# Last headed attention's opening re-ordered, its weights fetched by two queues, its output bias added by groups

## The chip, the cores and the metric

One core of a Trainium2 chip runs the whole program in one launch. The metric is the device time of one execution in microseconds (us), the median over several executions. Everything is in 32-bit floats where the text says nothing else.

## The reference, cut to what matters

The program is a stack of four layers on a stream of 2 x 1024 tokens of width 256. Each layer has a cross attention to 77 context tokens (or a self attention) and a feed-forward part. What is changed is the cross attention of the last layer, with 16 heads of 16, which reads a normalised copy of the stream and adds its result back:

```
def _L3_xattn_ref(q, k, v, mask, wq, bq, wk, bk, wv, bv, wo, bo):
    Q = (q @ wq + bq).reshape(b, s, 16, 16).transpose(0, 2, 1, 3)
    K = (k @ wk + bk)...            # k and v are the context, 77 tokens
    V = (v @ wv + bv)...
    score = jnp.einsum('bhqd,bhkd->bhqk', Q, K) / np.sqrt(16)
    score = jnp.where(mask, NEG, score)
    attn = jax.nn.softmax(score, axis=-1)
    x = jnp.einsum('bhqk,bhkd->bhqd', attn, V) ...
    return x @ wo + bo
...
x = x + _L3_xattn_ref(_layernorm(x, axis=-1), ctx_1024, ctx_1024, mask, ...)
x = x + _L3_ffn_ref(_layernorm(x, axis=-1), ...)     # 8 experts, each token goes to one
```

## The kernel before

The stream lies in SBUF as `x_resid`, 16 tiles of 128 tokens, in four groups of four tiles (`NCH` is 4, a group is 512 tokens). A stage is a block with one instruction stream for each engine. The streams are written out by hand, and semaphores tie them together. The page's engine names are PE (TensorE), DVE (VectorE), ACT (ScalarE), POOL (GpSimd) and SP (SyncE).

The stage before the change is the third layer's routed feed-forward. It ends with four DMAs on SP's queue that read the stream back into `x_resid`, one for each group (line 1970, 512 KB each).

The stage of the change is `headed_cross_attention` with the name `a3` (the page shortens its tensors to `a_...`). The same function serves the second layer, named `a1`, where there is a bias tensor instead of a mask, no arrivals and no projection bias. It has an opening and a loop over the 16 tiles. These are the steps of the opening before the change:

- SP's queue: `headed.fetch` issues the loads of `wk`, `wv`, two small selection tables, `bk`, `bv`, `bq`, `wq`, the mask (2048 rows of 77 bytes), `wo` and `bo` in that order, all counted on one semaphore. `w.wait` waits until all of them are in. Then come the next stage's small parameters, a wait for the four groups of the stream, and six loads of 1 MB each, the first three experts' weights (lines 395 and 396).
- PE: 16 matmuls that compute nothing that is used (`keep_busy`, line 76), `turn_tokens(0)` (transposes of group 0, line 1204), `w.wait`, the keys' projection (line 1251), `values(0)`, `turn_tokens(1)`, `values(1)`, `queries(0)` (line 1214), `turn_tokens(2)`, `queries(1)`, `scores(0)` (line 1224), `turn_tokens(3)`, `queries(2)`, `scores(1)`, `queries(3)`. A 32-bit matmul shows as two records, a transpose as one.
- DVE: statistics of the four groups (line 1019), `normed_tokens` (line 1009: subtract the mean, multiply by the root) of groups 0, 1 and 2, with `block_keys` (line 996), the evictions `tokens_turned` (line 1013) and `limits` (the mask turned into a limit, lines 1002 and 1003) between, `normed_tokens(3)`, then `scores` (line 1038) and `maxima` (line 1043) of tiles 0 and 1.
- POOL: four small copies and a memset, the roots of the variances by groups (lines 921 and 923), `w.wait`, for each of two batches the value bias (lines 934 to 940), then one addition of `bo` to all 16 tiles of `x_resid` (line 944), which waits until all 16 tiles are normed because the norm reads the same tensor, then `below_maximum(0)` (line 949).
- ACT: an exponential that warms its table (line 1136), evictions of transposes (1117), `w.wait`, evictions of values (1133, 1134) and of queries with their bias (1124).

The loop begins on PE with `scores(2)`, once the last query eviction on ACT is through and the six value steps on POOL are. For each tile it computes the scores two tiles ahead, transposes the exponentials, multiplies with the values and projects with `wo`. Its operations are untouched.

Of the kernel before, what the change touches and what calls it, by code (L numbers as in the profile page):

```python
# [5 lines left out]
ALU = mybir.AluOpType  # L6
# [5 lines left out]
U8 = mybir.dt.uint8  # L12
AX = mybir.AxisListType.X

P = 128
# [84 lines left out]
def bcast(ap, n):  # L100

    return ap.unsqueeze(0).broadcast_to([n] + list(ap.shape))
# [11 lines left out]
class Loads:  # L114
# [12 lines left out]
        self.at[n] = ap  # L127
        self.total += 16

    def fetch(self, eng, n, source):  # L130
        if self.target is None:
            self.counter[1] += self.total
            self.target = self.counter[1]
        eng.dma_start(self.at[n][:], source).then_inc(self.arrived, 16)

    def wait(self, eng):
# [659 lines left out]

class HeadedWeights:

    def __init__(self, core, ctx, name, counter, wqT, wkT, wvT, woT, mask=None, bq=None, bk=None, bv=None, bo=None):
        self.dram, self.loads = core.dram, Loads(core, ctx, name, counter)  # L800
        self.wqT, self.wkT, self.wvT, self.woT, self.mask = wqT, wkT, wvT, woT, mask
        self.bq, self.bk, self.bv, self.bo = bq, bk, bv, bo
        self.biased = bq is not None
        place = self.loads.place
        for n in ("wk", "wv", "wq", "wo"):
            place(n, [P, KD, D])
        place("head_of", [P, 8])
        place("rest_of", [8 * REST, 8])
        if self.biased:
            place("bq", [P, KD])  # L810
            place("bk", [P, KD])
            place("bv", [P, D])
            place("bo", [P, D])
        if mask is not None:
            place("mask", [P, NT, KEYS], U8)

    def fetch(self, sp):
        fetch = self.loads.fetch
        fetch(sp, "wk", self.wkT.rearrange("(k p) d -> p k d", p=P))
        fetch(sp, "wv", self.wvT.rearrange("(k p) d -> p k d", p=P))  # L820
        fetch(sp, "head_of", self.dram["head_of"])
        fetch(sp, "rest_of", self.dram["rest_of"])
        if self.biased:
            fetch(sp, "bk", self.bk)
            fetch(sp, "bv", bcast(self.bv, P))
            fetch(sp, "bq", self.bq)
        fetch(sp, "wq", self.wqT.rearrange("(k p) d -> p k d", p=P))
        if self.mask is not None:
            fetch(sp, "mask", self.mask.rearrange("(t p) k -> p t k", p=P))
        fetch(sp, "wo", self.woT.rearrange("(k p) d -> p k d", p=P))  # L830
        if self.biased:
            fetch(sp, "bo", bcast(self.bo, P))

    def wait(self, eng):
        self.loads.wait(eng)

    def __getitem__(self, n):
        return self.loads[n]


def headed_cross_attention(core, name, w, out, bias=None, arrivals=None, fetch=None, stream=None, experts=None, early=0):
# [8 lines left out]
    with ExitStack() as ctx:  # L850
# [59 lines left out]
        def _(pool):  # L910
# [6 lines left out]
            if arrivals is not None:  # L917
                for g in range(NCH):
                    own = slice(4 * g, 4 * g + 4)
                    pool.wait_ge(moments_done, 4 * g + 4)  # L920
                    pool.tensor_scalar(rstd[:, own], moments[:, own, 1], EPS, None, ALU.add).then_inc(eps_done, 1)
                    pool.wait_ge(eps_done, g + 1)
                    pool.tensor_tensor(rstd[:, own], rstd[:, own], half[:].broadcast_to([P, 4]), ALU.pow).then_inc(rstd_done, 1)
                pool.wait_ge(rstd_done, NCH)
# [16 lines left out]
            if projection_bias:  # L941
                pool.wait_ge(normed, NT)
                pool.wait_ge(v_sb, 3 * BATCH)
                pool.tensor_tensor(out[:], out[:], w["bo"][:].unsqueeze(1).broadcast_to([P, NT, D]), ALU.add).then_inc(biased, 1)

            def below_maximum(t):
                pool.wait_ge(max_done, t + 1)
# [14 lines left out]
            below_maximum(0)  # L962
            for t in range(NT):
                if t + 1 < NT:
                    below_maximum(t + 1)
# [12 lines left out]
        def _(dve):  # L978
# [6 lines left out]
                dve.wait_ge(chain, count[0])  # L985

            def block_keys():
                w.wait(dve)
                link(dve.tensor_reduce(quarter_of[:], head_of[:].rearrange("p (j h) -> p h j", h=2), AX, ALU.max))
                link(dve.tensor_scalar(quarter_of[:], quarter_of[:], DK ** -0.5, None, ALU.mult))  # L990
                dve.wait_ge(kv_mm, 1)
                for k in range(KD):
                    keys = ps[:, k, 0:W].rearrange("p (b n) -> p b n", b=BATCH)
                    for h in range(2):
                        if projection_bias:
                            dve.tensor_scalar(kbd[:, :, k, h, :], keys, bkT[:, k:k + 1], quarter_of[:, h:h + 1], ALU.add, ALU.mult).then_inc(kbd_done, 1)
                        else:
                            dve.tensor_scalar(kbd[:, :, k, h, :], keys, quarter_of[:, h:h + 1], None, ALU.mult).then_inc(kbd_done, 1)

            def limits():  # L1000
# [69 lines left out]
                dve.bn_aggr(moments[:, t, :], stats[:, t, :]).then_inc(out_moments, 1)  # L1070

            if arrivals is not None:
                for g in range(NCH):
                    statistics(g)
            normed_tokens(0)
            normed_tokens(1)
            tokens_turned(0)
            normed_tokens(2)
            block_keys()
            tokens_turned(1)  # L1080
            limits()
            normed_tokens(3)
            tokens_turned(2)
            scores(0)
            maxima(0)
            tokens_turned(3)
            scores(1)
            maxima(1)
# [25 lines left out]
        def _(act):  # L1114
# [13 lines left out]
            def values(b):  # L1128
# [57 lines left out]
        def _(pe):  # L1186
# [60 lines left out]
            turn_tokens(0)  # L1247
            w.wait(pe)
            for k2 in range(KD):
                for k in range(KD):  # L1250
                    mm = pe.matmul(ps[:, k2, 0:W], w["wk"][:, k, k2 * P:(k2 + 1) * P], core.ctxT[:, k, :], start=(k == 0), stop=(k == KD - 1))
            mm.then_inc(kv_mm, 1)
            values(0)
            turn_tokens(1)
            values(1)
            queries(0)
            turn_tokens(2)
            queries(1)
            pe.wait_ge(kbd_done, 2 * KD)
            pe.wait_ge(v_raw, 3 * BATCH)  # L1260
            scores(0)
            turn_tokens(3)
            queries(2)
            scores(1)
# [1703 lines left out]
def program(nc, dram):  # L2968
    with ExitStack() as ctx:
# [46 lines left out]
        with ExitStack() as routed:  # L3016
# [2 lines left out]
            experts.keep(routed, 3)  # L3019
            with ExitStack() as layer:  # L3020
                headed = HeadedWeights(core, layer, "a3", "a0o", *(dram[f"L3_w{n}"] for n in "qkvo"), mask=dram["mask_bf"],
                                       bq=dram["L3_bq"], bk=dram["L3_bk"], bv=dram["L3_bv"], bo=dram["L3_bo"])
                headed.fetch(nc.sync)
# [93 lines left out]
```

## Time and profile before

| | us |
|---|---|
| median of 3 runs (2120.34 to 2125.79) | 2125.45 |
| profiled execution, its own time | 2126.2 |
| its span | 2124.4 |
| PE busy | 1987.4 |
| this stage's opening, from PE's first instruction to its loop | 1821.77 to 1858.81 |

Times in the trace count from the start of the span. A row of the timeline gives the start, the length, the engine, the line, what is written and what is read, and in brackets how long the engine had been idle and what released it. DMA rows on a queue (SPq) give the time that the issue took, not the transfer.

### The profile page before, as it was taken

To read this page: it belongs to the slowest core of one execution; us is meant where nothing else is said; L and a number is where in the kernel's file an instruction comes from. 1 tells how busy PE (TensorE), PEld (TensorE's weight loads), DVE (VectorE), ACT (ScalarE), POOL (GpSimd) and SP (SyncE) were. 2 spreads that over 40 slices of the span, in tenths; PEclk is the share of its full clock that TensorE was granted. 3 is DMA by queue.
4 is the path that set the end of the run, shared out by engine and by line. 5 is a ranking of instruction groups with operands and counts; after the bars stand their busy time and mean duration, and the time that the engine had idled before them with its cause. 6 is when DMAs were issued, how large, how long until landed. Compare 5 with 4: busy or idle time off the path is not lost. (4 is left out here: it accounts for less than half of the span.)

```text
span 2124.4 us, 39759 instructions
## 1 busy us (share of the span) xinstructions
PE 1987.4 (94%) x12589; PEld 1455.5 (69%) x12590; DVE 1047.7 (49%) x2419; ACT 931.7 (44%) x1932; POOL 722.1 (34%) x814
## 2 busy tenths in 40 slices
PE   6899999988999999879999978999999999798998
PEld 5576656742333232469999867999999999565898
DVE  6885853677777777353222255222222222487221
ACT  2422652157777777523333332333333333265222
POOL 0122973520000000234333342434333343585433
PEclk9999999999999999999999988999999999999999
DMA  5003300042111112155222164522222222602721
GB/s 171 21 1 129 124 13 0 1 155 72 39 43 48 45 39 60 63 178 168 32 33 35 27 206 145 147 35 34 33 36 38 35 33 32 191 22 62 232 35 23
DMA packets 124860, 150.44 MB, mean 71 GB/s; under 512 B 27638, under 2 KB 105303, under 8 KB 124749
## 3 DMA queue, kind: packets, MB, share of 16 engines
q1 hardware_dynamic: 93981, 116.61, 17.0%
q0 software_dynamic: 24288, 31.81, 9.4%
q8 instruction: 64, 1.05, 0.2%
q10 hardware_dynamic: 6480, 0.59, 0.2%
q14 instruction: 47, 0.39, 0.1%
HBM read 113.33 MB, written 37.38 MB: 71 GB/s over the span
## 5 line engine op out<-in xcount | busy, mean ns | idle before, releaser
L2102 PE MATMUL banks<-m_rowsT,x_normT 128*128 128x128 f32 x4032 | 471.2, 275 | 4.5 <-ACT m_hT L2341 2.0
L2102 PEld LDWEIGHTS banks<-m_rowsT,x_normT 128*128 128x128 f32 x4032 | 461.8, 192 | 18.9 <-ACT m_hT L2341 2.4
L2111 PE MATMUL banks<-m_experts,m_hT 128*128 x2016 | 455.8, 380 | 0.0
L2111 PEld LDWEIGHTS banks<-m_experts,m_hT 128*128 128x128 f32 x2016 | 374.0, 190 | 45.2
L2341 ACT ACTIVATE m_hT<-banks,m_bias 128x128 f32<-128x128 f32 x848 | 241.7, 368 | 245.0 <-PE banks L2102 241.3
L2017 POOL DMA_INDIRECT scratch_acc<-m_y,m_row_ids x106 | 170.2, 1606 | 398.2 <-ACT m_y L2351 357.4
L2812 ACT ACTIVATE sh_pT<-banks 128x1024 f32<-128x1024 f32 x256 | 250.8, 1024 | 27.0 <-PE banks L2773 27.0
L2290 DVE COPY m_rowsT<-banks 128x256 f32<-128x256 f32 x88 | 37.4, 425 | 409.7 <-PE banks L2093 409.7
L2351 ACT ACTIVATE m_y<-banks,m_weight 128x256 f32<-128x256 f32 x126 | 59.6, 473 | 351.8 <-PE banks L2114 289.0
L2836 DVE TENSOR_REDUCE sh_mhalf<-banks 128x1 f32<-128x512 f32 x308 | 194.3, 684 | 36.4 <-PE banks L2722 36.4
L2274 DVE TENSOR_SCALAR x_normT<-m_experts 128x2048 f32 x129 | 168.1, 1303 | 74.0 <-issue 69.5
L2773 PE MATMUL banks<-sa_qs,sa_ks 99*128 99x512 bf16 x512 | 153.8, 385 | 9.7 <-ACT sh_pT L2812 7.5
L2004 POOL DMA_INDIRECT m_rows<-scratch_rows,m_row_ids x114 | 127.1, 1115 | 99.2 <-POOL m_row_ids L2001 97.0
L2713 POOL TENSOR_TENSOR x_norm<-x_norm,sp_bo 128x256 f32<-128x256 f32 x16 | 11.6, 724 | 389.6 <-DVE sh_m L2846 389.6
L2722 PE MATMUL banks<-sa_ks,sa_qs 96*128 96x512 bf16 x410 | 136.0, 387 | 0.0
L2763 PE MATMUL banks<-sh_pT,sa_vh 128*17 128x512 f32 x1024 | 132.1, 598 | 1.2 <-ACT sh_pT L2812 1.2
L76 PE MATMUL banks<-ident 128*128 128x256 f32 x336 | 92.9, 429 | 32.4 <-PEq L1847 18.0
L2773 PEld LDWEIGHTS banks<-sa_qs,sa_ks 99*128 99x128 bf16 x512 | 41.5, 98 | 116.7 <-ACT sh_pT L2812 51.0
L2286 DVE TENSOR_SCALAR m_rowsT<-banks,m1p_gain,m1p_shift 128x128 f32<-128x128 f32 x76 | 27.7, 406 | 177.1 <-PE banks L2093 177.1
L76 PEld LDWEIGHTS banks<-ident 128*128 128x128 f32 x336 | 70.7, 218 | 47.6 <-issue 35.5
L2722 PEld LDWEIGHTS banks<-sa_ks,sa_qs 96*128 96x128 bf16 x410 | 40.3, 98 | 77.0 <-DVE sh_mhalf L2836 35.6
L2841 DVE CUSTOM_DVE_ANT_0 sh_rise<-banks,sh_rise 128x512 f32<-128x512 f32 x102 | 68.4, 689 | 34.5 <-ACT sh_rise L2800 33.3
(413 smaller groups left out, 2766.5 us busy)
## 6 DMA issues: line engine op xcount, KB each, us to landing
m_experts<-L_W SPq DMA_DIRECT2D x32, 1024.0 KB
m_experts<-L1f_W SPq DMA_DIRECT2D x16, 1024.0 KB
a_bt<-bias SPq DMA_DIRECT2D x16, 616.0 KB, 3.8
scratch_parts<-sp_part SPq DMA_DIRECT2D x16, 384.0 KB, 2.5
sa_qs<-scratch_parts SPq DMA_DIRECT2D x96, 64.0 KB, 2.3
scratch_rows<-x_norm SPq DMA_DIRECT2D x12, 512.0 KB, 3.9
sa_ks<-scratch_parts SPq DMA_DIRECT2D x90, 64.0 KB, 2.3
scratch_acc<-x_resid SPq DMA_DIRECT2D x8, 512.0 KB, 2.9
```

The source lines that it names most:

```text
L76: pe.matmul(self.ps[:, bank, 0:2 * P], self.ident[:], self.ident[:].unsqueeze(1).broadcast_to([P, 2, P]), start=True, stop=True)
L2004: pool.indirect_dma_start(rows[:, w % RING, :], None, table, bass.IndirectOffsetOnAxis(ap=row_ids[:, w:w + 1], axis=0), bounds_check=TOK, ...
L2017: pool.indirect_dma_start(stream, bass.IndirectOffsetOnAxis(ap=row_ids[:, w:w + 1], axis=0), y[:, w % RING, :], None, bounds_check=TOK - 1 ...
L2102: mm = pe.matmul(ps[:, H_BANK[u] + f // 4, f % 4 * P:(f % 4 + 1) * P], w1_tile[:, u, k, f * P:(f + 1) * P], rowsT[:, u, k, :], start=(k == ...
L2111: mm = pe.matmul(ps[:, Y_BANK[u], 0:D], hT[:, u, f, :], experts.w2[:, bass.ds(slot_of(e), 1), f, :], start=(f == 0), stop=(f == FB - 1 and ...
L2274: ins = dve.tensor_scalar(w1_tile[:, u, :, :], experts.w1[:, bass.ds(slot_of(e), 1), :, :].rearrange("p e k f -> p (e k) f"), 0.0, None, A ...
L2341: ins = act.activation(hT[:, u, f, :], ps[:, H_BANK[u] + c, j * P:(j + 1) * P], func, bias=bias[:, u, f:f + 1])
L2722: pe.matmul(ps[:, bank["a", s, c], :], qs[u][0:SR, h, t * P:(t + 1) * P], keys, start=True, stop=True).then_inc(a_mm, 1)
L2763: mm = pe.matmul(ps[32 * g:32 * g + DK + 1, O_BANK, :], vh[:, b * KT + k, head, :], pT[:, (2 * k + h) % 4, half, :], start=(k == 0), stop= ...
L2773: mm = pe.matmul(ps[:, B_BANK + 2 * (n % 2) + half, :], ks[u][:, h, k * P:(k + 1) * P], qs[u][:, h, half * CH:(half + 1) * CH], start=True ...
L2812: act.activation(pT[:, n % 4, :, :], ps[:, B_BANK + 2 * (n % 2):B_BANK + 2 * (n % 2) + 2, :], ACT.Exp, scale=DK ** -0.5).then_inc(exp_done, 1)
L2836: dve.tensor_reduce(mhalf[:, s % 2, half, col:col + 1], ps[:, bank["a", s, c], :], AX, ALU.max).then_inc(a_max, 1)
```

## The change

`HeadedWeights` now holds two sets. The set of the keys (`wk`, `wv`, the two tables, `bk`, `bv`) stays on SP's queue; the others (`wq`, `bq`, the mask, `wo`, `bo`) are issued by ACT, ahead of its table load, and are counted on a second semaphore (`others="a0v"`). `expect` sets a set's target without issuing. For the second layer both sets stay on SP with one semaphore, and its order is kept.

```diff
+    def wait_of_keys(self, eng):
+        (self.others if self.together else self.of_keys).wait(eng)
...
             def limits():
+                w.wait(dve)
...
-            w.wait(pool)
-            for b in range(BATCH):
+            def values(b):
...
-                pool.tensor_tensor(out[:], out[:], w["bo"][:]....broadcast_to([P, NT, D]), ALU.add).then_inc(biased, 1)
+            def add_output_bias(g):
+                own = slice(4 * g, 4 * g + 4)
+                pool.wait_ge(normed, 4 * g + 4)
+                pool.tensor_tensor(out[:, own], out[:, own], w["bo"][:]....broadcast_to([P, 4, D]), ALU.add).then_inc(biased, 1)
...
+                roots(0)
+                roots(1)
+                roots(2)
+                w.wait_of_keys(pool)
+                w.wait(pool)
+                add_output_bias(0)
+                values(0)
+                roots(3)
+                add_output_bias(1)
+                add_output_bias(2)
+                add_output_bias(3)
+                below_maximum(0)
+                values(1)
```

DVE's opening in this stage (`block_keys` waits for the keys' set alone):

```diff
-                for g in range(NCH):
-                    statistics(g)
-            normed_tokens(0)
...
+                statistics(0)
+                statistics(1)
+                normed_tokens(0)
+                statistics(2)
+                tokens_turned(0)
+                normed_tokens(1)
+                block_keys()
+                statistics(3)
+                tokens_turned(1)
+                normed_tokens(2)
+                normed_tokens(3)
+                limits()
+                tokens_turned(2)
+                scores(0)
+                maxima(0)
+                scores(1)
+                maxima(1)
+                tokens_turned(3)
...
-                dve.wait_ge(biased, 1)
+                dve.wait_ge(biased, NCH)
```

ACT and PE:

```diff
+            if arrivals is not None:
+                w.fetch_others(act)
             act.activation(warm[:], half[:], ACT.Exp)
             tokens_turned(0)
-            w.wait(act)
             values(0)
             tokens_turned(1)
             values(1)
+            w.wait(act)
             queries(0)
...
-            core.keep_busy(pe, 7, 16 if arrivals is not None else 5)
...
+                core.keep_busy(pe, 7, 10)
+                keys()
+                turn_tokens(0)
+                values(0)
+                turn_tokens(1)
+                values(1)
+                w.wait(pe)
+                queries(0)
+                turn_tokens(2)
+                pe.wait_ge(q_sb, KD)
+                pe.wait_ge(kbd_done, 2 * KD)
+                pe.wait_ge(v_raw, 3 * BATCH)
+                scores(0)
+                queries(1)
+                turn_tokens(3)
+                scores(1)
+                queries(2)
...
             queries(3)
```

`keys()` is the former keys' projection with a wait for the keys' set alone. In `program`, `headed.fetch(nc.sync)` becomes `headed.fetch_of_keys(nc.sync)` and `headed.others.expect()`.

## Rows read from the trace of the kernel before

**Rows 1.** The page, busy time of each engine and its share of the span.
```profile
PE 1987.4 (94%) x12589; PEld 1455.5 (69%) x12590; DVE 1047.7 (49%) x2419; ACT 931.7 (44%) x1932; POOL 722.1 (34%) x814
```

**Rows 2.** Windows: stretch, length, busy time by engine, granted clock, DMA share, GB/s.
```profile
1834.12:1857.07 22.95, 22.95 (x112) 13.41 (x112) 14.78 (x23) 8.26 (x16) 17.61 (x11) 1.00 0.77 274
...
1858.81:1945.13 86.32, 79.61 (x800) 53.80 (x800) 66.34 (x138) 54.31 (x110) 76.18 (x69) 1.00 0.06 20
```

**Rows 3.** Timeline of PE and of ACT's last query evictions in the opening.
```profile
1821.77 9.84 PE L76 MATMUL banks<-ident 128*128 128x256 f32 x32 [9.93 <-PEq L1847]
...
1831.45 1.04 PE L1204 MATMUL banks<-ident,x_norm 128*128 128x128 f32 x8
...
1834.12 1.32 PE L1251 MATMUL banks<-ctxT_sb,a_wk 128*128 128x154 f32 x8 [1.64 <-DMA a_bo<-L_bo]
...
1853.37 3.70 PE L1214 MATMUL banks<-x_normT,a_wq 128*128 128x512 f32 x8
...
1857.51 1.24 ACT L1124 ACTIVATE a_qT<-banks,a_bq 128x512 f32<-128x512 f32 x2
1858.81 0.81 PE L1224 MATMUL banks<-a_kbd,a_qT 32*128 32x154 f32 x16 [1.74 <-ACT a_qT L1124]
```

**Rows 4.** Timeline of the queue of SP.
```profile
1826.39 4.01 SPq L134 DMA_DIRECT2D a_wo<-L_wo  x1
...
1832.06 0.37 SPq L395 DMA_DIRECT2D m_experts<-L_W  x1
```

**Rows 5.** Windows of the reload and the weights, columns as in rows 2.
```profile
1821.73:1831.61 9.88, 9.84 (x34) 8.23 (x35) 8.37 (x39) 1.49 (x2) 7.08 (x13) 0.72 1.15 304
...
1826.50:1827.00 0.50, 0.50 (x2) 0.35 (x2) 0.50 (x2) 0.00 (x0) 0.33 (x2) 0.50 1.11 348
...
1830.00:1830.50 0.50, 0.50 (x4) 0.45 (x3) 0.50 (x3) 0.00 (x0) 0.42 (x2) 1.00 1.54 129
```

**Rows 6.** Line 2437, issues by ACT: ns min/median/max, first and last start.
```profile
L2437 ACTq DMA_DIRECT2D sa_ks<-scratch_parts x6: 357/1143/1208, 472.5 to 477.6; - x6
```

**Rows 7.** Timeline of DVE in the opening.
```profile
1823.24 1.41 DVE L1019 BATCH_NORM_STATS2 stats<-x_resid 128x6 f32<-128x256 f32 x4 [23.21 <-DMA x_resid<-scratch_acc]
...
1833.13 1.37 DVE L1009 TENSOR_SCALAR x_norm<-x_resid,moments,rstd 128x256 f32<-128x256 f32 x4
...
1838.68 0.79 DVE L1002 TENSOR_SCALAR a_bt<-a_mask 128x1232 f32<-128x1232 uint8 x1
...
1841.13 2.53 DVE L1009 TENSOR_SCALAR x_norm<-x_resid,moments,rstd 128x256 f32<-128x256 f32 x4
...
1848.31 1.51 DVE L1038 TENSOR_TENSOR a_s<-banks,a_bt 128x616 f32<-128x616 f32 x2 [3.51 <-PE banks L1224]
1849.85 1.44 DVE L1043 TENSOR_REDUCE a_mx<-a_s 128x16 f32<-128x1232 f32 x1
1851.21 0.68 DVE L1013 COPY x_normT<-banks 128x512 f32<-128x512 f32 x1
```

**Rows 8.** Timeline of POOL in the opening.
```profile
1829.72 0.30 POOL L921 TENSOR_SCALAR rstd<-moments 128x4 f32<-128x4 f32 x1 [0.22 <-DVE moments L1022]
1830.11 1.16 POOL L923 TENSOR_TENSOR rstd<-rstd,minus_half 128x4 f32<-128x4 f32 x1
1838.36 1.44 POOL L934 TENSOR_TENSOR a_v_main<-a_v_main,a_bv 64x128 f32<-64x128 f32 x2 [7.09 <-ACT a_v_rest L1134]
1839.87 1.80 POOL L937 TENSOR_TENSOR a_v_rest<-a_v_rest,a_bv 104x256 f32<-104x256 f32 x1
...
1842.52 0.99 POOL L934 TENSOR_TENSOR a_v_main<-a_v_main,a_bv 64x128 f32<-64x128 f32 x2
1845.16 8.87 POOL L944 TENSOR_TENSOR x_resid<-x_resid,a_bo 128x4096 f32<-128x4096 f32 x1
1853.98 2.25 POOL L949 TENSOR_TENSOR a_s<-a_s,a_mx 128x1232 f32<-128x1232 f32 x1
```

**Rows 9.** A window ahead of the stage, columns as in rows 2.
```profile
1816.50:1817.00 0.50, 0.00 (x0) 0.00 (x0) 0.00 (x0) 0.00 (x0) 0.00 (x0) 0.99 1.14 76
```

More of the change, by code:

```diff
@@ L797, with __init__ @@
 class HeadedWeights:
-    def __init__(self, core, ctx, name, counter, wqT, wkT, wvT, woT, mask=None, bq=None, bk=None, bv=None, bo=None):
-        self.dram, self.loads = core.dram, Loads(core, ctx, name, counter)
+    def __init__(self, core, ctx, name, counter, wqT, wkT, wvT, woT, mask=None, bq=None, bk=None, bv=None, bo=None, others=None):
+        self.dram, self.of_keys, self.others = core.dram, Loads(core, ctx, name, counter), Loads(core, ctx, f"{name}o", others or counter)
         self.wqT, self.wkT, self.wvT, self.woT, self.mask = wqT, wkT, wvT, woT, mask
@@ L802, in __init__ @@
         self.bq, self.bk, self.bv, self.bo = bq, bk, bv, bo
[L803 to L808, printed above, removed]
+        self.biased, self.together = bq is not None, others is None
+        self.of_keys.place("wk", [P, KD, D])
+        self.of_keys.place("wv", [P, KD, D])
+        self.others.place("wq", [P, KD, D])
+        self.others.place("wo", [P, KD, D])
@@ L809, in __init__ @@
+        self.of_keys.place("head_of", [P, 8])
+        self.of_keys.place("rest_of", [8 * REST, 8])
         if self.biased:
[L810 to L813, printed above, removed]
+            self.others.place("bq", [P, KD])
+            self.of_keys.place("bk", [P, KD])
+            self.of_keys.place("bv", [P, D])
+            self.others.place("bo", [P, D])
         if mask is not None:
-            place("mask", [P, NT, KEYS], U8)
@@ L817, in fetch @@
[L817 to L822, printed above, removed]
-        if self.biased:
[L824 to L827, printed above, removed]
+            self.others.place("mask", [P, NT, KEYS], U8)
@@ new lines, in fetch_of_keys, with fetch_others @@
+    def fetch_of_keys(self, eng):
+        fetch = self.of_keys.fetch
+        fetch(eng, "wk", self.wkT.rearrange("(k p) d -> p k d", p=P))
+        fetch(eng, "wv", self.wvT.rearrange("(k p) d -> p k d", p=P))
+        fetch(eng, "head_of", self.dram["head_of"])
+        fetch(eng, "rest_of", self.dram["rest_of"])
+        if self.biased:
+            fetch(eng, "bk", self.bk)
+            fetch(eng, "bv", bcast(self.bv, P))
+    def fetch_others(self, eng):
+        fetch = self.others.fetch
+        fetch(eng, "wq", self.wqT.rearrange("(k p) d -> p k d", p=P))
+        if self.biased:
+            fetch(eng, "bq", self.bq)
@@ L834, in wait @@
     def wait(self, eng):
-        self.loads.wait(eng)
+        self.others.wait(eng)
+    def wait_of_keys(self, eng):
+        (self.others if self.together else self.of_keys).wait(eng)
     def __getitem__(self, n):
-        return self.loads[n]
+        return self.of_keys[n] if n in self.of_keys.at else self.others[n]
 def headed_cross_attention(core, name, w, out, bias=None, arrivals=None, fetch=None, stream=None, experts=None, early=0):
@@ L916, in _, with roots @@
             pool.wait_ge(zeros_done, 1)
-            if arrivals is not None:
-                for g in range(NCH):
[L919 to L924, printed above, removed]
-            w.wait(pool)
-            for b in range(BATCH):
+            def roots(g):
+                own = slice(4 * g, 4 * g + 4)
+                pool.wait_ge(moments_done, 4 * g + 4)
+                pool.tensor_scalar(rstd[:, own], moments[:, own, 1], EPS, None, ALU.add).then_inc(eps_done, 1)
+                pool.wait_ge(eps_done, g + 1)
+                pool.tensor_tensor(rstd[:, own], rstd[:, own], half[:].broadcast_to([P, 4]), ALU.pow).then_inc(rstd_done, 1)
+            def values(b):
                 pool.wait_ge(v_raw, 3 * b + 3)
@@ L1072, in _ @@
             if arrivals is not None:
-                for g in range(NCH):
-                    statistics(g)
-            normed_tokens(0)
[L1076 to L1088, printed above, removed]
+                statistics(0)
[16 more added lines that the diff above has]
+                tokens_turned(3)
+            else:
+                normed_tokens(0)
+                normed_tokens(1)
+                tokens_turned(0)
+                normed_tokens(2)
+                block_keys()
+                tokens_turned(1)
+                limits()
+                normed_tokens(3)
+                tokens_turned(2)
+                scores(0)
+                maxima(0)
+                tokens_turned(3)
+                scores(1)
+                maxima(1)
             if projection_bias:
-                dve.wait_ge(biased, 1)
+                dve.wait_ge(biased, NCH)
             dve.wait_ge(normed, NT)
@@ L1244, in project, with keys @@
                 mm.then_inc(y_mm, 1)
-            core.keep_busy(pe, 7, 16 if arrivals is not None else 5)
[L1247 to L1264, printed above, removed]
+            def keys():
+                w.wait_of_keys(pe)
+                for k2 in range(KD):
+                    for k in range(KD):
+                        mm = pe.matmul(ps[:, k2, 0:W], w["wk"][:, k, k2 * P:(k2 + 1) * P], core.ctxT[:, k, :], start=(k == 0), stop=(k == KD - 1))
+                mm.then_inc(kv_mm, 1)
+            if arrivals is not None:
+                core.keep_busy(pe, 7, 10)
+                keys()
+                turn_tokens(0)
+                values(0)
+                turn_tokens(1)
+                values(1)
+                w.wait(pe)
[4 more added lines that the diff above has]
+                pe.wait_ge(v_raw, 3 * BATCH)
+                scores(0)
+                queries(1)
+                turn_tokens(3)
+                scores(1)
+                queries(2)
+            else:
+                core.keep_busy(pe, 7, 5)
+                turn_tokens(0)
+                keys()
+                values(0)
+                turn_tokens(1)
+                values(1)
+                w.wait(pe)
+                queries(0)
+                turn_tokens(2)
+                queries(1)
+                pe.wait_ge(kbd_done, 2 * KD)
+                pe.wait_ge(v_raw, 3 * BATCH)
+                scores(0)
+                turn_tokens(3)
+                queries(2)
+                scores(1)
             queries(3)
```

31 lines of the change are left out of this document (19 added, 12 removed).

## The prediction

> **What bounds the kernel now.** I read the page's first part, then windows over this stage, then the timelines of its opening, PE first. TensorE is busy 94% of the span [rows 1], so outside its own work time is lost only where it idles or does filler. The changed function's second-layer use keeps its order and its single queue, so I cost it at nothing. The last layer's loop takes 86.32 us for 16 tiles with PE busy 79.61 and POOL 76.18 [rows 2]. Its operations do not change, so it moves as a block with the moment at which it begins, PE at 1858.81 [rows 3]. The question is how much earlier that moment comes.
>
> Three stretches lie before it. From 1821.77 PE does 9.84 us of filler and from 1831.45 the first transposes; then it waits until 1834.12, with the last weights load (`bo`) as releaser [rows 3]. From 1834.12 to 1857.07 it is busy 22.95 of 22.95 us [rows 2]. Last, 1.74 us pass while ACT evicts the last queries, 1857.51 to 1858.75, behind the first exponential [rows 3]. So the opening is bound first by the arrival of the weights and then by PE's own chain of projections. The 8.87 us addition of the bias on POOL [rows 8] sits beside that chain; it holds the first maximum's subtraction to 1853.98 though the maximum was there at 1851.29 [rows 7, 8], but PE was busy meanwhile. What it cost is the end: the exponential late on ACT put the last query evictions some 0.4 us back.
>
> **The weights' arrival.** Before, everything waited for `bo`. SP's issue of `wo` stood for 4.01 us behind the mask's, so `bo` was issued at about 1830.4 [rows 4] and in at 1834.1. Now the keys' set is ahead of nothing else on its queue, and PE, DVE and POOL begin the keys and values when it is in; I call that time A. The others' arrival is B.
>
> The transfers, by sizes of the code: the reload is 2.10 MB, of which some 1.9 MB are to come at 1821.7; the keys' set is 0.66 MB, the others 0.65 MB and the mask 0.16 MB in 2048 rows. While long rows move the rate is 348 GB/s with the DMA engines at 1.11, their full share; in the half microsecond from 1830.00, where the mask is on, it is 129 GB/s at 1.54 [rows 5]: the engines are full and move little. At 304 GB/s over 1821.73 to 1831.61 [rows 5] the engines have no spare time for a second queue to fill.
>
> Bounds for A: with the SP queue served alone, 2.56 MB at 348 GB/s take 7.4 us: 1829.1. With the whole of the other queue served before it is through, 3.21 MB take 9.2 us and the mask about 2.5 (my reading of the slow stretch that starts at 1830.0): 1833.4. I take the middle, A = 1831.5, a little late because the other queue starts at the same time and has few bytes. Bounds for B: not before the keys' set has made way, 1832.5. Late, if the rest of it shares the engines with the 1 MB loads: SP no longer stands at `wo`, so it issues these as soon as the four stream groups are in, some 3 us before the 1832.06 of now [rows 4]; then `wo` and `bo`, 24 rows for each of the 16 engines, each pay for a 4 KB row of the experts beside them (348 / 16 = 22 GB/s for an engine, so 0.19 us; their own 1 KB row is 0.05): 24 x 0.24 = 5.6 us after about 1832.5, so 1838. I take B = 1834.5.
>
> The skill bears on this. The rows show full DMA engines from 1821.7 on. The Trainium skill, page "DMA: Bandwidth & Descriptors", section "Issuing engines are not separate DMA queues", says that transfers issued by different engines run on the same 16 DMA engines and interleave, so that a second issuer saves only the time of issuing. By that rule the second queue shortens the whole load by no more than SP's 4.01 us stand, and takes bandwidth from the keys' set. It is the ground of the first rival below; the trace agrees as to the full engines.
>
> **The chain from A.** PE: the 22.95 us of now, plus the first transposes, which stood before the wait and now stand behind it (1.04 us for one group alone, some 0.9 in the pipelined chain) [rows 2, 3]: 23.85. Moving scores and transposes about adds nothing to this sum. Waits that are new in it: `turn_tokens(1)` needs the norm of group 1 (1.37 us [rows 7]), which DVE now does after evicting group 0 (0.7); PE has `values(0)` (about 1.8) as cover, so 0.1 to 0.3 us show. The last queries need DVE's eviction of group 3, now behind `maxima(1)`: about 0.5 us. After PE's end ACT's second eviction of 0.69 us and a handoff, 0.75. The filler is cut from 32 records to 20 and ends near 1829 (at half clock until 1827.1, then about 0.24 us each), so it does not hold A back. Sum: A + 23.85 + 0.8 + 0.75 = A + 25.4, which gives 1856.9.
>
> **The chain from B.** POOL now has, behind `w.wait`: the first bias group, values(0), and only then `roots(3)`, which DVE's last norm waits for. Prices: a quarter of 8.87 is 2.2; the values took 4.16 for the first batch (1838.36 to 1842.52) and 2.64 for the second (1842.52 to 1845.16) [rows 8]. The first ran beside DVE's mask work, its 1.80 us step above all; I take 3.0 and keep both ends. The root is 1.55 from its first step (1829.72 to 1831.27), 1.4 taken without its wait. The norm of group 3 is 1.37 alone and 2.53 beside POOL's additions [rows 7]; POOL goes on to bias group 1 then, so I take 1.6 and keep 2.53 as an end. Then DVE: limits 2.45 (1838.68 to 1841.13), turned 0.7, scores 1.51, maxima 1.44, scores 1.51, maxima 1.44, turned 0.7 [rows 7]. Up to there 2.2 + 3.0 + 1.4 + 1.6 + 2.45 + 0.7 + 5.9 + 0.7 = 17.95. Then PE's last queries 3.7 [rows 3] less the overlap with the eviction, and the eviction, 4.3. With handoffs B + 22.4, which gives 1856.9 too. So both chains end together, and either can decide.
>
> The rest costs nothing or nearly. The bias additions of groups 1 to 3 (6.6 us) lie between `roots(3)` and the first maximum; by this sum they end near 1847.5 and the maximum comes near 1848.5, so DVE covers them by about 1 us. If DVE slows them like the 1.80 step, subtraction and second values shift by up to 2 us, and the values' end at about 1855 still stands before the loop's begin. ACT's five issues take 0.36 to 1.2 us each [rows 6], 6 us at most, then the table load and warm-up (1.5); if the issue of `wo` stands its 4.01 us there as well, ACT is free at about 1833.2. Its first eviction is due at A + 2.2 = 1833.7, so the cover just holds; without it the cost is at most 1 us. The stage's small parameters and the six expert loads get issued earlier and are needed after 1945. The extra waits (`limits`, four instead of one for the bias) have nothing new behind them but what the B chain counts.
>
> **The sum.** The loop starts at 1856.9 instead of 1858.81: 1.9 us gained. The profiled execution took 2126.2 (span 2124.4), which would become 2124.3; it was 0.75 above the median of the runs, 2125.45, so I forecast 2123.5.
>
> **Rivals.** (1) The queues only share: A is 1833.4, as if one queue carried both. Then A + 25.4 = 1858.8, no change, 2125.4. For it: full engines [rows 5]. Against it: the mask's slow rows now lie on the other queue. (2) Full gain: the keys are in with the filler's end, 1829, and B is before 1832. Then 1854.4, a gain of 4.4, 2121.0. For it: SP's queue is a chain of long rows with the keys directly behind the reload. Against: ACT issues from 1821.7 too. (3) Slower: the others are late. Mechanism: `wo` and `bo` on ACT's queue compete with the experts' 4 KB rows, POOL stands at its wait with `roots(3)` behind it, and DVE's last norm and the scores come after that. It decides from B = 1836.4 on, where B + 22.4 passes 1858.81; at B = 1838 it is +1.6 us, and with both slow prices of the contended POOL and DVE steps (1.2 + 0.9) +3.7: 2127.1 to 2129.2. For it: SP issues the experts 3 us sooner and the wait is for all five loads. Against: the others have few bytes and start with the reload. In sentences of its own: the skill's page "DMA: Bandwidth & Descriptors", section "Queues, rings and completion order", has each DMA engine go round between its queues by packets, not bytes. By that rule short rows beside long ones lose, the mask's above all, and B is 1837 or later; that no row shows two such queues at once leaves it a rival. (4) The clock: with the filler ending at 1829, PE idles until A. The granted clock was still 0.99 between 1816.5 and 1817.0 [rows 9], 5 us after PE's last work (its idle before 1821.77 was 9.93 [rows 3]); so a gap of 2.5 us should not lower it, and one of 4.4 might. At half clock the next 3 us of PE work would cost some 3 more.
>
> **How the numbers follow.** The forecast 0.42, rival 1 0.17, rival 2 0.18, rival 3 0.20, rival 4 0.03. The likeliest time is 2123.5. The range holds the full gain and the slow side's lower part with the spread of the runs themselves (5.45 us over three): 2119.0 to 2128.0. What can be told from no change is about 0.3%, 6.4 us. None of the cases reaches that on the fast side (the largest gain is 4.5), so only the spread of the runs gives faster 0.11; slower 0.05 needs B beyond 1842 or rival 4 on top of 3. Within 0.3%: 0.84.
>
> **What would show it.** The changed kernel's first key projection on PE gives A (its releaser should be a load of the keys' set); POOL's first bias group gives B. `bo` in pieces of 2.2 us; the loop's first scores near 1856.9 on the old time scale, 35.1 us after PE's first filler; DVE's last norm right behind a root. Wrong would be: a wait on PE or ACT in the chain that I don't name, POOL's additions longer than 2.5 us each, a granted clock below 1 after 1829, or a loop that no longer takes 86 us.

## Result: 0.3% slower, and the profile after

The changed kernel took 2133.02 us (median of 20 runs, 2126.56 to 2139.25) against 2127.67 us (20 runs, 2120.34 to 2132.50): ratio 1.003, 95% interval 1.002 to 1.0039. I had forecast 2123.5, with 2119.0 to 2128.0 as range and slower by more than 0.3% at 0.05.

Single executions spread by 5 us and more, so the profiles are compared by the opening alone: from PE's first filler to the loop's first scores. It was 37.04 us before (1821.77 to 1858.81, [rows 3]) and is 43.66 us after (1827.58 to 1871.24), 6.62 longer. The span grew by 13.1 us; of that 5.81 lie before the stage, whose instructions are the same, and 0.7 after the opening. Nothing makes the 5.81 the work of this change: the stage began at 1823.20 in a second profile of the changed kernel (e8), and anywhere from 1817.73 to 1827.58 in the thirteen profiles of this document. The loop took 86.9 us before and after. The medians differ by 5.35, and the interval of the ratio stands for 4.3 to 8.3 us, so it holds the 6.62.

The timeline of the changed kernel's opening, with the rows that answer to [rows 3, 7, 8]:

```profile
1827.58 7.55 PE L76 MATMUL banks<-ident 128*128 128x256 f32 x20 [9.93 <-PEq L1922]
1829.05 5.67 ACTq L137 DMA_DIRECT2D a3o_wo<-L_wo  x1
1834.62 0.38 SPq L398 DMA_DIRECT2D m_experts<-L_W  x1
1837.92 1.32 PE L1302 MATMUL banks<-ctxT_sb,a_wk 128*128 128x154 f32 x8 [2.79 <-DMA a_bv<-L_bv]
1842.39 2.37 POOL L958 TENSOR_TENSOR x_resid<-x_resid,a3o_bo 128x1024 f32<-128x1024 f32 x1 [5.50 <-issue]
1847.52 1.05 POOL L937 TENSOR_TENSOR rstd<-rstd,minus_half 128x4 f32<-128x4 f32 x1
1848.54 4.71 POOL L958 TENSOR_TENSOR x_resid<-x_resid,a3o_bo 128x1024 f32<-128x1024 f32 x2
1848.60 5.45 DVE L1042 TENSOR_SCALAR x_norm<-x_resid,moments,rstd 128x256 f32<-128x256 f32 x4 [0.61 <-POOL rstd L937]
1853.98 0.79 DVE L1035 TENSOR_SCALAR a_bt<-a3o_mask 128x1232 f32<-128x1232 uint8 x1
1854.13 2.83 POOL L958 TENSOR_TENSOR x_resid<-x_resid,a3o_bo 128x1024 f32<-128x1024 f32 x1 [0.88 <-DVE x_norm L1042]
1854.80 3.46 DVE L1036 SCALAR_TENSOR_TENSOR a_bt<-a3o_mask,a_bt 128x1232 f32<-128x1232 uint8 x1
1858.29 0.69 DVE L1046 COPY x_normT<-banks 128x512 f32<-128x512 f32 x1
1858.90 1.50 DVE L1071 TENSOR_TENSOR a_s<-banks,a_bt 128x616 f32<-128x616 f32 x2
1859.13 1.94 PE L1256 MATMUL banks<-ident,x_norm 128*128 128x128 f32 x8 [5.45 <-DVE x_normT L1046]
1861.00 1.41 PE L1276 MATMUL banks<-a_kbd,a_qT 32*128 32x154 f32 x16
1862.34 8.12 PE L1266 MATMUL banks<-x_normT,a3o_wq 128*128 128x512 f32 x16
1871.24 0.81 PE L1276 MATMUL banks<-a_kbd,a_qT 32*128 32x154 f32 x16 [0.78 <-ACT a_qT L1174]
```

See first the two rows that begin at 1848.5: POOL's bias additions of groups 1 and 2, and DVE's four norms of group 3, which take 5.45 us and not 1.37 as alone [rows 7]. Then 1854: the third addition, and the limits' second step of 3.46 us. PE waited 5.45 us for the eviction behind them. Before, that step took 1.58 us, beside POOL's value steps, one of which in turn took 1.80 us [rows 8] where the same step of the second batch took 0.73:

```profile
1839.51 1.58 DVE L1003 SCALAR_TENSOR_TENSOR a_bt<-a_mask,a_bt 128x1232 f32<-128x1232 uint8 x1
1843.58 0.73 POOL L937 TENSOR_TENSOR a_v_rest<-a_v_rest,a_bv 104x256 f32<-104x256 f32 x1
```

The view of the norm's line, and the timeline in two narrow windows, say how the 5.45 us of the changed kernel are made up:

```profile
L1042 DVE TENSOR_SCALAR x_norm<-x_resid,moments,rstd x16: 400/407/2446, 1832.5 to 1853.7; 128x256 f32<-128x256 f32 x16
1848.60 2.45 DVE L1042 TENSOR_SCALAR x_norm<-x_resid,moments,rstd 128x256 f32<-128x256 f32 x1 [0.61 <-POOL rstd L937]
1850.97 2.44 DVE L1042 TENSOR_SCALAR x_norm<-x_resid,moments,rstd 128x256 f32<-128x256 f32 x1
```

(The first row is in ns: min, median, max.) Two of the four norms took 2.45 and 2.44 us, one beside each of the two POOL additions of 2.35 us, and ended 0.1 to 0.2 us behind it. The other two came behind them, about 0.3 us each. Windows of 1 us over PE's idle time (columns as in rows 2) show what followed: the granted clock goes from 1.00 to 0.50, the lower of its two levels (1.2 GHz), and comes back in 1864.

```profile
1856.00:1857.00 1.00, 0.00 (x0) 0.00 (x0) 1.00 (x1) 0.00 (x0) 0.96 (x1) 1.00 0.07 23
1857.00:1858.00 1.00, 0.00 (x0) 0.00 (x0) 1.00 (x1) 0.00 (x0) 0.00 (x0) 0.77 0.01 3
1858.00:1859.00 1.00, 0.00 (x0) 0.00 (x0) 0.96 (x3) 0.00 (x0) 0.00 (x0) 0.50 0.00 0
...
1864.00:1865.00 1.00, 1.00 (x3) 0.46 (x2) 0.98 (x1) 0.00 (x0) 0.92 (x3) 0.82 0.00 0
```

Times from PE's first filler, in us (the forecast's on the same scale):

| | before | forecast | changed | e5 | e6 | e7 |
|---|---|---|---|---|---|---|
| keys' projection starts (A) | 12.35 | 9.7 | 10.34 | 8.59 | 8.48 | 8.65 |
| first bias group starts (B) | 23.39, whole | 12.7 | 14.81 | 12.40 | 12.35 | 21.21 |
| norms of group 3 take | 2.53 | 1.6 | 5.45 | 6.75 with group 2 | 2.67 with group 2 | 2.26 |
| loop's first scores | 37.04 | 35.1 | 43.66 | 41.43 | 35.95 | 33.30 |

### The profile page after: what moved, and what is told of

Read it like the earlier page. It is cut to its first block and busy times, and to the rows that moved or that the text cites. A ratio compares the mean times of both kernels' runs of the same rounds, so it can differ in the third digit from the quotient of the medians.

```text
span 2137.5 us, 39736 instructions
## 1 busy us (share of the span) xinstructions
PE 1994.7 (93%) x12574; PEld 1461.8 (68%) x12578; DVE 1054.0 (49%) x2419; ACT 932.4 (44%) x1932; POOL 720.7 (34%) x817
## 5 line engine op out<-in xcount | busy, mean ns | idle before, releaser
L76 PEld LDWEIGHTS banks<-ident 128*128 128x128 f32 x324 | 68.7, 220 | 47.5 <-issue 35.5
```

The source lines that it names most:

```text
L76: pe.matmul(self.ps[:, bank, 0:2 * P], self.ident[:], self.ident[:].unsqueeze(1).broadcast_to([P, 2, P]), start=True, stop=True)
```

## Experiments

Each kernel up to e9 ran once, so its own time says little (2124.42 to 2137.34 us for the nine); what is compared is the opening in its profile.

**e1: overlap taken away.** POOL's groups 1 to 3 come after DVE's limits.

```diff
                 roots(3)
+                pool.wait_ge(xT_dve, 3)
                 add_output_bias(1)
```

> The opening, from PE's first filler to the loop's first scores, took 37.04 us before and 43.66 us in the changed kernel. Here POOL adds the bias of groups 1 to 3 only after DVE has evicted the turned tokens of group 2, so after its last norms and the limits. Theory 1 (DVE's norms and limits stand still while a POOL addition of 2.4 us runs): the norms of group 3 fall from 5.45 us to about 1.4, the limits from 4.28 (0.79 + 3.46) to 2.4, PE's idle of 5.45 us before the last transposes goes, with it the fall of the clock, and the opening is 37 to 38 us, with POOL's additions now the last thing before the first subtraction. Rival (DVE is slowed by the experts' loads that stream into SBUF in the same microseconds): norms and limits stay at 5.4 and 4.3 us and the opening gets longer than 43.7.

```profile
1835.39 2.14 DVE L1023 TENSOR_SCALAR a_quarter_of<-a_quarter_of 128x2 f32<-128x2 f32 x1
...
1841.12 2.66 DVE L1043 TENSOR_SCALAR x_norm<-x_resid,moments,rstd 128x256 f32<-128x256 f32 x8
...
1844.53 1.44 DVE L1037 SCALAR_TENSOR_TENSOR a_bt<-a3o_mask,a_bt 128x1232 f32<-128x1232 uint8 x1
1846.78 7.00 POOL L958 TENSOR_TENSOR x_resid<-x_resid,a3o_bo 128x1024 f32<-128x1024 f32 x3 [4.57 <-DVE x_normT L1047]
```

Eight norms in 2.66 us, the limits' second step 1.44. The opening was 39.10 us, 4.56 less, somewhat above the 37 to 38 expected: its keys ran in 1.97 us and not 1.32, at half clock: the filler had ended at 6.43 us, PE was idle 3.70 ahead of them, and the granted clock fell to 0.50 half a microsecond after they had begun. And its first bias group came 0.8 later. The experts' loads ran beside the norms as before (367 to 409 GB/s from 1841 to 1845), so they are not the cause. The first row is a step that nobody had in view: a DVE step on two elements for each partition, 0.17 us in the changed kernel, took 2.14 us here, because it fell into the first bias group (1835.07 to 1837.51) and ended with it.

**e3: one long addition.** The bias in one instruction after `roots(3)`, behind all 16 norms.

```diff
-                add_output_bias(0)
                 values(0)
                 roots(3)
-                add_output_bias(1)
-                add_output_bias(2)
-                add_output_bias(3)
+                pool.wait_ge(normed, NT)
+                pool.tensor_tensor(out[:], out[:], w["bo"][:]....broadcast_to([P, NT, D]), ALU.add).then_inc(biased, NCH)
```

> The changed kernel with the output bias as one addition of 8.9 us again, after the values of batch 0 and the last root, and once all 16 tiles are normed. Theory 1 (a DVE step with 32-bit or 8-bit SBUF operands waits until the running POOL instruction is through): the norms of group 3 take 1.4 us, POOL starts its addition with DVE's limits, and the limits take 9 to 10 us instead of 4.28: the opening is 41 to 43 us. Rival (both engines share a port's time evenly): the limits take at most double, below 5 us, and the opening is 38 to 39 us.

```profile
1843.23 1.38 DVE L1040 TENSOR_SCALAR x_norm<-x_resid,moments,rstd 128x256 f32<-128x256 f32 x4 [0.61 <-POOL rstd L937]
...
1844.76 9.24 POOL L985 TENSOR_TENSOR x_resid<-x_resid,a3o_bo 128x4096 f32<-128x4096 f32 x1 [1.56 <-DVE x_norm L1040]
1845.36 9.95 DVE L1034 SCALAR_TENSOR_TENSOR a_bt<-a3o_mask,a_bt 128x1232 f32<-128x1232 uint8 x1
```

The norms are at 1.38, and the limits' second step takes 9.95 us, until 1.3 us after POOL's one instruction ends: it stood for the whole of it. Even sharing is out. Nor is a tensor in common the cause: the step reads the mask and writes the limits, the addition touches neither. The mechanism is as expected; the opening, 46.51, was above the 41 to 43. The standing came to 8.4 us, the others' set was in only 17.00 us after the filler's start (POOL's first value step, released by the load of `bo`), 2.2 later than in the changed kernel, and PE, idle for 7.80 us, lost its clock again.

**e9: short additions.** Each group as four additions of one tile.

```diff
-                pool.tensor_tensor(out[:, own], out[:, own], ...).then_inc(biased, 1)
+                for t in range(4 * g, 4 * g + 4):
+                    pool.tensor_tensor(out[:, t], out[:, t], w["bo"][:], ALU.add).then_inc(biased, 1)
...
-                dve.wait_ge(biased, NCH)
+                dve.wait_ge(biased, NT)
```

> The changed kernel with each bias group added as four additions of one tile (128 x 256), each 0.72 us long instead of one of 2.35. If a DVE step waits until the running POOL instruction is through, the wait shrinks with the instruction: the last four norms, 5.45 us now, take 3.5 to 4.2 us (each 0.3 and up to 0.72 of wait), and the limits' second step 1.6 to 2.4 instead of 3.46. If instead the two engines share the port by time, it is the sum of POOL's work that counts, and both stay where they are or grow, since the 16 pieces are longer in sum (11.6 us against 9.4). Opening by the first 41 to 43, by the second 45 or more, with the keys at 10.1 to 10.5 us in both.

```profile
1843.86 10.20 POOL L959 TENSOR_TENSOR x_resid<-x_resid,a3o_bo 128x256 f32<-128x256 f32 x12
1843.92 3.01 DVE L1043 TENSOR_SCALAR x_norm<-x_resid,moments,rstd 128x256 f32<-128x256 f32 x4 [1.24 <-POOL rstd L937]
...
1848.21 1.84 DVE L1037 SCALAR_TENSOR_TENSOR a_bt<-a3o_mask,a_bt 128x1232 f32<-128x1232 uint8 x1
```

More POOL time in sum (12.99 us for 9.91) and less harm: 3.01 us for the four norms, less than the 3.5 expected at best, and the longest single one 880 ns. The limits' second step took 1.84, as expected. Part of the added POOL time is POOL's own standing: a piece of 0.72 us took 1.27 and another 1.92 where they met the two steps of the limits (1.33 and 1.84). The opening fell to 40.46, below the expected 41, with the first bias group at 15.60. What DVE loses goes with the length of one POOL instruction. The Trainium skill, page "SBUF — State Buffer", section "Who interferes with whom", says just this: VectorE and GpSimd share one pair of SBUF ports, an exclusive lock held for a whole instruction, wanted by a `tensor_scalar` in a two-port mode or by a VectorE step with two SBUF inputs. No run here shows which mode a norm is in. The traces agree for the norms and for the limits' second step, and also where no lock is due: the scores, with one input in PSUM, took 1.51 us beside the 8.87 us addition before the change [rows 7, 8].

**e4: experts after the opening.**

```diff
+                sp.wait_ge(exp_done, 1)
                 for e in range(early):
                     experts.fetch(sp, e)
```

> The changed kernel with SP's six expert loads held back until the first exponential, so that they stream after the opening. It tells two things apart. The others' arrival: POOL's first bias group starts 14.8 us after PE's first filler now; if the experts' 4 KB rows hold up the output weights and bias (my rival 3), it comes at 12.5 to 13.5 us and the norms of group 3 start 1.3 to 2 us earlier; if not, it stays at 14.8. DVE's slow steps: theory 1 keeps the norms of group 3 above 4 us and the limits above 3.5; if the loads into SBUF were the cause, they fall to 1.4 and 2.4 us. Opening by theory 1 about 42, by the other 37.

```profile
1831.48 1.32 PE L1303 MATMUL banks<-ctxT_sb,a_wk 128*128 128x154 f32 x8 [2.78 <-DMA a_bv<-L_bv]
1833.34 2.36 POOL L959 TENSOR_TENSOR x_resid<-x_resid,a3o_bo 128x1024 f32<-128x1024 f32 x1 [2.88 <-issue]
1834.31 2.74 DVE L1043 TENSOR_SCALAR x_norm<-x_resid,moments,rstd 128x256 f32<-128x256 f32 x4
1841.06 6.74 DVE L1043 TENSOR_SCALAR x_norm<-x_resid,moments,rstd 128x256 f32<-128x256 f32 x8
```

Counted from its filler (1821.17) the keys start at 10.31, as in the changed kernel, but the first bias group at 12.17 and not 14.81. So the experts' loads do hold up the others' set, by 2.6 us, and not the keys'. The norms stay slow without a byte moving. The opening, 43.34, gained only 0.3 and not the 1.7 expected: the earlier first group now stands in the way of group 1's norms (2.74 for 1.37), and PE waits 1.72 us for them.

**e5: one queue.** Both sets on SP, two semaphores.

```diff
-            if arrivals is not None:
-                w.fetch_others(act)
...
-                headed.fetch_of_keys(nc.sync)
-                headed.others.expect()
+                headed.fetch(nc.sync)
```

> The changed kernel with both sets issued by SP again, the keys' set first, and still two semaphores. Times from PE's first filler. The keys' projection starts at 10.3 us in the changed kernel, POOL's first bias group at 14.8 to 17.1. If the second queue's rows are what holds the keys up, the keys start at 7.6 to 8.3 here, and if the experts' rows held up the output weights, the first bias group starts at 12.4 to 13 (all loads are in at about 12.3 as before the change, and the experts come behind them on the same queue). DVE's norms and limits still run into POOL's additions, 5 and 4 us, so the opening ends at 40 to 42 us and not at the 37 of before. Rival (one queue is slower, since SP's 4 us stand is back): keys at 10 or later.

```profile
1830.31 1.32 PE L1300 MATMUL banks<-ctxT_sb,a_wk 128*128 128x154 f32 x8 [1.10 <-DMA a_bv<-L_bv]
...
1834.12 2.34 POOL L958 TENSOR_TENSOR x_resid<-x_resid,a3o_bo 128x1024 f32<-128x1024 f32 x1 [3.29 <-issue]
```

From its filler (1821.72) the keys come at 8.59, 1.7 us sooner than with two queues and a little later than I expected, and the first bias group at 12.40. The opening, 41.43, is inside the expected 40 to 42. The second queue brought the keys nothing. One queue with a semaphore for each set has the keys 3.8 us sooner than the 12.35 of before; the shorter filler and the keys ahead of the first transposes are part of that, since PE's filler and transposes alone lasted 10.7 us there.

**e6: e5 with e1's wait**, and **e11, the same kernel timed.**

> e5 with e1's wait as well: one queue, and POOL's bias groups 1 to 3 only behind DVE's limits and the eviction of group 2. If arrival and overlap are the two causes and the filler's cut costs nothing once the keys come early (idle below 1 us ahead of them, clock stays up), the opening is 35.5 to 36.5 us, below the 37.04 of before; what then stands last is POOL's chain of three additions, first subtraction and values of batch 1. If the re-ordering costs something else, it stays above 37.

The opening was 35.95 us, inside the expected 35.5 to 36.5. Overlap costs 5.5 us here (41.43 to 35.95).

> The kernel of e6 timed against the one before. Its opening was 35.95 us, 1.1 less than before, 7.7 less than the changed kernel's: ratio 0.9995 with an interval that holds 1; if something outside the opening got slower in this change, the ratio would be 1.001 or more for e10 and e11 alike.

Ratio to the kernel before 0.9998, interval 0.9984 to 1.0012 (12 runs against 23). It holds the 0.9995 expected; a loss of up to 0.1% outside the opening is not excluded by it, but no sign of one is seen. Its profile is a second execution of e6: opening 36.00.

**e2: filler against the clock's fall.**

```diff
                 queries(1)
+                pe.wait_ge(q_sb, KD + 1)
+                core.keep_busy(pe, 6, 11)
                 turn_tokens(3)
```

> The changed kernel with 11 more filler matmuls on PE (5.2 us) ahead of the last transposes, in the bank of the queries, so that PE is not idle there. It isolates the cost of the clock's fall (granted clock 0.50 from 1857.3 to 1864.3). If half clock costs what the longer records say (last transposes 1.94 against 1.09, scores 1.41 against 0.81, queries 8.12 for two groups against 7.2), the opening falls from 43.66 to about 41.3 us. If those matmuls are bound by DVE and ACT anyway, it stays above 43.

```profile
1845.45 4.91 PE L76 MATMUL banks<-ident 128*128 128x256 f32 x22
...
1852.53 1.06 PE L1256 MATMUL banks<-ident,x_norm 128*128 128x128 f32 x8 [2.17 <-DVE x_normT L1046]
1853.85 0.81 PE L1276 MATMUL banks<-a_kbd,a_qT 32*128 32x154 f32 x16 [0.26 <-DVE a_s L1071]
```

The clock held, transposes and scores ran at full speed, and the opening was 44.57, longer, which I had not expected: its first bias group came at 17.07 and not 14.81. From that group to the loop it is 27.50 against 28.85, and up to the end of the limits the two are alike (15.87 us from that group in both), so the clock's fall costs 1.3 us of the opening, not 2.4; the rest DVE's chain would have taken anyway.

**e8: the changed kernel again.**

> The changed kernel itself once more, for the spread of its opening: 43.66 us in its profile. The keys' start was 10.1 to 10.3 us in four profiles of kernels with its queues, the first bias group's 14.8 to 17.1 where the experts run beside it. If the opening follows that group, it comes at 43.7 to 46 us, with 28.9 us from the group's start to the loop.

Keys 10.49 (at half clock, 2.18 us), first bias group 15.69, opening 45.77, within the range expected. But from that group to the loop it is 30.08 us and not 28.9: the keys' late end put group 1's norms beside the first bias group, where they took 3.64 us for 1.37, and PE waited 2.62 for them. So the changed kernel's opening depends on when the others' set is in (14.81 to 17.07 us in the six profiles with its loads: changed, e1, e2, e3, e8, e9) and on which DVE step POOL's additions then meet.

**e7: another order from these findings**, and **e10, the same kernel timed.** One queue, two semaphores; PE as changed; the limits ahead of the last norms; no bias addition before the last norm. The queue's edit is that of e5; statements are joined here by semicolons.

```diff
 DVE:            statistics(0); statistics(1); normed_tokens(0); statistics(2)
-                tokens_turned(0); normed_tokens(1); block_keys(); statistics(3)
-                tokens_turned(1); normed_tokens(2); normed_tokens(3); limits()
-                tokens_turned(2); scores(0); maxima(0); scores(1); maxima(1); tokens_turned(3)
+                statistics(3); normed_tokens(1); tokens_turned(0); block_keys()
+                tokens_turned(1); normed_tokens(2); limits(); normed_tokens(3)
+                tokens_turned(2); scores(0); maxima(0); tokens_turned(3); scores(1); maxima(1)
 POOL:           roots(0); roots(1); roots(2)
-                w.wait_of_keys(pool); w.wait(pool); add_output_bias(0); values(0); roots(3)
-                add_output_bias(1); add_output_bias(2); add_output_bias(3); below_maximum(0); values(1)
+                roots(3); w.wait_of_keys(pool); values(0); values(1); w.wait(pool)
+                pool.wait_ge(normed, NT)
+                add_output_bias(0); add_output_bias(1); below_maximum(0)
+                add_output_bias(2); add_output_bias(3)
```

> A version made from the findings: one queue and two semaphores as e5, PE's order of the changed kernel, DVE with the statistics of all groups and the norms of 0 and 1 ahead of the first eviction, the limits ahead of the last norm and group 3 evicted ahead of scores 1, POOL with the four roots first, both values, then the bias groups only when all 16 tiles are normed, the first subtraction between groups 1 and 2. By theory 1 nothing on DVE runs longer than alone but beside POOL's values (one step of up to 1 us), PE's chain from the keys at 7.6 us is 24 to 25 us, and the opening is 32.5 to 34.5 us, 3 us or so less than before. If POOL's chain (values, 9 us of additions, two subtractions) is the bound it is 35.

```profile
1840.04 1.58 DVE L1037 SCALAR_TENSOR_TENSOR a_bt<-a3o_mask,a_bt 128x1232 f32<-128x1232 uint8 x1
1841.65 2.26 DVE L1043 TENSOR_SCALAR x_norm<-x_resid,moments,rstd 128x256 f32<-128x256 f32 x4
...
1844.04 4.69 POOL L958 TENSOR_TENSOR x_resid<-x_resid,a3o_bo 128x1024 f32<-128x1024 f32 x2 [0.60 <-issue]
1847.48 0.81 PE L1275 MATMUL banks<-a_kbd,a_qT 32*128 32x154 f32 x16
1850.89 4.67 POOL L958 TENSOR_TENSOR x_resid<-x_resid,a3o_bo 128x1024 f32<-128x1024 f32 x2
1856.13 0.81 PE L1275 MATMUL banks<-a_kbd,a_qT 32*128 32x154 f32 x16 [0.78 <-ACT a_qT L1175]
```

Opening 33.30 us as expected, 3.74 less than before, though the keys came at 8.65 and not at 7.6. The two steps shown are not quite free of POOL: beside its value steps the norms took 2.26 for 1.37, and two value steps took 2.65 where two take 0.99 alone.

> The kernel of e7 timed against the one before. Its opening was 33.30 us in its profile, 3.74 less than before (37.04), so the ratio should be 0.998 (3.7 of 2127 us), if the rest of the program does not change; the spread of the runs outside the opening (5 us between executions) may hide it in a single pair.

2124.15 us (12 runs) against 2128.55 (23 runs), ratio 0.9984, interval 0.9971 to 0.9998: the 0.998 expected, and just clear of no change. The changed kernel's interval, 1.002 to 1.0039, lies on the other side. Its profile is a second execution of e7: opening 33.33.

## Why the prediction was wrong

The step that failed is the price of DVE's work beside POOL's additions in the chain from B. I had both signs before me. The norms at 2.53 instead of 1.37 beside POOL's 1 us steps, and POOL's 1.80 beside DVE's limits, were read as a mild mutual slowing, with 2.53 as the upper end. As e3 and e9 show, they were waits for one another's whole instructions, and the change sets 2.4 us instructions there. The page "SBUF — State Buffer" of the Trainium skill, section "Who interferes with whom", states that rule; I did not weigh it.

The late B alone would not have made the kernel slower: by my own sum, B + 22.4, it gives 37.2 for the 37.04 of before. The other 6.4 us or so came behind it.

From the forecast 35.1 to 43.66, by the terms of that chain:

- B: 14.81 for 12.7, +2.1. My rival 3 named the mechanism, and e4 shows it (12.17 without the experts' traffic). Its weight, 0.20, was too low, and its price left out the overlap behind it.
- First group, values and root: 6.2 (1842.39 to 1848.60) for 6.6, -0.4.
- Norms of group 3: 5.45 for 1.6, +3.85.
- Limits: 4.3 (1853.98 to 1858.29) for 2.45, +1.85.
- From there to the loop: 12.95 for 11.75, +1.2. e2 puts the clock's part at 1.3. My rival 4 had the clock, but ahead of the keys; in e8 and e1 it fell there, in the profile of the changed kernel only ahead of the last transposes.

The sum is +8.6 of the 8.56 found.

Right were: the loop moved as a block, and what follows the opening took 265.6 us before and 266.3 after; A within 0.7 us; the reading that PE waited for `bo`, as e5 shows with the same queue; the chain from B as the one that can decide; ACT's issues hidden (its table load ended at 1836.9, PE's first transposes at 1840.1), although the issue of `wo` stood for 5.67 us there.

Wrong besides: what the second queue takes from the keys I put at "a little". e5 shows one queue with two semaphores 1.7 us better at the keys and 2.4 at the others, so that A at 10.34 was near my number partly by luck: one queue alone gave 8.59, where my bound was 7.4. This is as the rule of the Trainium skill, page "DMA: Bandwidth & Descriptors", section "Issuing engines are not separate DMA queues", which I had quoted, would have it: the second issuer brought neither set in sooner. And cutting the filler was called free. It was, with the keys at 10.3 us and the filler's end at 7.5. In e1 and e8 the filler ended at 6.4 and 6.5, and the keys ran at half clock. In e10 and e11 it ended there too, but with one queue the keys came at 8.7 and 8.5, behind 2.21 and 2.01 us of idle time, and ran at full clock.

Only argued: why the others' set came as late as 17.0 us in two profiles (e2, e3) and at 14.8 to 15.7 in the other four. The two queues' sharing would do it, and e4 shows the experts' part, but no run separates the mask's rows.

## What to carry to other kernels

Before POOL work is moved beside DVE work, look at each DVE step for itself. Here the norms and the mask's second step, all from SBUF to SBUF, could stand for the whole of POOL's running instruction. The statistics (1.39 us beside a bias group of 2.37, 1.37 to 1.41 before), the maxima (1.44), the scores (1.51) and the evictions from PSUM (0.68, these three beside the 8.87 us addition [rows 7, 8]) did not. Place long POOL instructions beside the latter, or cut them into short ones. To start early on part of a load, give it its own semaphore and the head of the queue that is there (keys at 8.59 us). A second queue had them at 10.34, and what the first queue sent next held the second one's set up by 2.6 us (e4).

## What was not expected of the hardware

A DVE step of 1.44 us (alone, in e1) took 9.95 beside one POOL instruction of 9.24, and one of 0.17 took 2.14 beside a POOL instruction of 2.44. The bias in quarters made two norms of about 0.3 us take 2.45 and 2.44; in sixteenths no norm took more than 0.88. POOL's additions were hardly slowed, 2.35 to 2.84 us for a quarter, but its short steps were: a value step took 1.80 for 0.73 before the change, two took 2.65 for 0.99 in e7, and a sixteenth of the bias 1.92 for 0.72 in e9.

PE's granted clock fell to 0.50 within 0.6 us behind the gap of 3.70 us (e1) and 3.98 us (e8) ahead of the keys, and not behind the gaps of 2.72 to 2.79 there. That makes no rule for other places: ahead of the last transposes, with other work before, it fell behind gaps of 2.73 (e9), 2.90 (e8) and 2.91 us (e4), and not behind one of 2.53 (e5).
